# A two-layer cross-attention kernel: a new order inside each beat on all engines, with the transposes of the probabilities ahead of the next scores

## The chip, the cores and the metric

The kernel runs on one core of one Trainium2 chip. The metric is the device time of one execution in microseconds (us).

## The reference

`x` is (64, 128, 160) and `ctx` (64, 77, 256), in fp32. Layer 0 is a transformer block with 20 heads of 64 columns, layer 1 an attention with 20 heads of 8 columns and four image tokens:

```
n = LN1(x);  x = x + attn(n, n)            # a = 0: 128 keys
n = LN2(x);  x = x + attn(n, ctx)          # a = 1: 77 keys
x = (h_a * gelu(h_g)) @ w2 + b2 + x        # h = LN3(x) @ w1 + b1, 640 + 640 columns
# layer 1, context split in 73 text and 4 image tokens:
P = softmax(q k_text / sqrt(8));  text = P v_text
sem = l2norm(P @ text_ctx) . l2norm(image_ctx)
ip = softmax(q k_ip / sqrt(8) + 0.5 sem) * mask @ v_ip
out = (text + ip) @ W_out + b_out + x
```

## The kernel before

The batch is cut into 16 groups (GROUPS) of four batch elements (GB), and each group into two halves (h) of two. In layer 0 a unit n is one pair of heads of one half: n = 0 to 19 are the 128-key attention, 20 to 39 the 77-key one. Two units make a duo d, so a group has 20 duos, and each duo has one **beat**. A beat has three slots t (STEP = 60 slots for a group); every engine runs the same loop `for t in range(FIRST, LAST)` over slots, with `beat, sub = divmod(t, 3)` (`part` on TensorE), and waits only on semaphores. In beat B TensorE transposes the probabilities of duo B (`probs_transposed`), makes the scores of duo B+1 (`scores`), the products with v of duo B-1 (`probs_v`) and the out-projection of duo B-1 (`wo`), and the queries of duo B+2. Layer 1 is cut into 20 units a group too, each of four heads, and one runs in each beat, about one group behind (L1_BEAT): `scores1`, `probs_transposed1`, `probs_v1` on TensorE, `exp1` and `pt1_out` on ScalarE, `softmax1_in` and `unit_out` on VectorE, `norms_of` on GpSimd.

Softmax of a duo: `softmax_in` (VectorE, maximum from PS, L1231), `exp` twice (ScalarE, L977, eight activations in all), `prob_sums` twice (VectorE, L1248 and L1253), `normalise` twice (GpSimd, L1433), transposes (TensorE, L793), `pt_out` (ScalarE, L965). `scores1` writes bank 1 of PT and `probs_transposed1` bank 0, the same two banks that `probs_transposed` fills; so the latter waits for `exp1_done` and `pts1_done`.

Everything else is a **job**: it takes one of the two banks of PG in turn and waits until the job two before it has been read out:

```
if JOB[name] >= len(PG):
    pe.wait_ge(*read_out(JOBS[JOB[name] - len(PG)]))
ps = bank(name)
```

Jobs of every beat are two `qk` (queries, and keys for a = 0; read out by ScalarE, L913) and one `v` (read out by VectorE). Jobs at slots of their own are `xT` (transposes of a norm's output, L659, into nT), `cT` (of the context, L653), `kc` (context keys), `ff` (a feed-forward tile: Gelu on ScalarE, L922, then h on VectorE, L1175), `down`, `q1`, `k1`, `vip`, `ctx1`, and `ipT`, `ip`, `oT1`, `y` at the end of each layer-1 batch element. Their slots stand in tables written by hand at the top (NORM_SLOT for statistics of norm k, half h; FF_SLOT, DOWN_SLOT, Q1_SLOT, PREP_SLOT for the context). Negative slots lie in the group before, those from 60 on in the group behind. SyncE issues all loads in the order of the slots: slices of weights (`load_slice`), stacks, `load_context`, `load_x`.

Of the kernel before, what the change touches and what calls it, by code (L numbers as in the profile page):

```python
# [5 lines left out]
def xattn_program(nc: bass.Bass, D, out: bass.AP):  # L6
    fp32 = mybir.dt.float32
# [55 lines left out]
    FIRST_NORM_SLOT = {(0, 0): -14}  # L63
    VIP_SLOT = 56
    K1_SLOT = (46, 49)
    K1_STACK = 56
    CTX1_SLOT = {0: 59, 1: 74, 2: 89, 3: 104}

    ctx = ExitStack()
    with ctx:  # L70
# [44 lines left out]
        cin, gl = shared[0:TS, :, :], shared[:, :, :]  # L115
# [14 lines left out]
        kx = keys_full[:, :].rearrange("p (a n) -> p a n", a=NP)  # L130
        SE = sb("SE", [128, 4, 512])
# [37 lines left out]
        csq = k1_hi[0:TS, 0, :, :].rearrange("p b t -> p (b t)")[:, 0:E].bitcast(fp32)  # L169
# [184 lines left out]
        def norm_slot(g, k, h):  # L354
            own = FIRST_NORM_SLOT if g == 0 else {}
            return STEP * g + own.get((k, h), NORM_SLOT[(k, h)])

# [5 lines left out]
        tails_at = slots((tail_slot(g, b) + d, (g, b, d)) for g in range(GROUPS) for b in range(GB) for d in range(-1, 9))  # L363

        contexts_at = slots((max(FIRST, STEP * g + (PREP_SLOT[0] + 4 if h else FF_SLOT[-1] + 1 - STEP)), (g, h))
                            for g in range(GROUPS) for h in range(2))
# [14 lines left out]
            + [(tail_slot(g, b) + d, (kind, g, b)) for d, kind in ((5, "ipT"), (6, "ip"), (7, "oT1"), (8, "y"))  # L381
# [86 lines left out]
        with nc.Block() as block:  # L468
# [7 lines left out]
            def _(sp):  # L476
                def load_context(g, h):
                    if h == 0 and g >= 1:
                        sp.wait_ge(S["h_done"], NTH[("ff", g - 1, 2 * F - 1)])
                    elif h == 1:  # L480
                        sp.wait_ge(S["job_full"], JOB[("cT", g, 0)] + 1)
# [57 lines left out]
                for t in range(FIRST, LAST):  # L539
# [40 lines left out]
                    for g, b, d in tails_at(t - 1):  # L580
                        if d == 8:
                            store(g, b)
# [8 lines left out]
            def _(pe):  # L591
# [271 lines left out]
                for t in range(FIRST, LAST):  # L863
                    beat, part = divmod(t, 3)
                    turned, multiplied = min(max(beat + 1, 0), DUOS * GROUPS), min(max(beat, 0), DUOS * GROUPS)
                    if part == 0:
                        if duo_at(beat + 1):
                            scores(*duo_at(beat + 1))
                        if duo_at(beat):
                            probs_transposed(*duo_at(beat))  # L870
                        if duo_at(beat - 1):
                            probs_v(*duo_at(beat - 1))
                    for name in qk_at(t):
                        job(name)
                    for name in late_at(t):
                        if name[0] == "v":
                            job(name)
                    if part == 1 and l1_at(beat - 1):
                        probs_transposed1(*l1_at(beat - 1), turned)
                    if part == 1 and l1_at(beat):  # L880
                        scores1(*l1_at(beat), turned)
                    if part == 2 and duo_at(beat - 1):
                        g, d = duo_at(beat - 1)
                        wo(g, 2 * d)
                        wo(g, 2 * d + 1)
                    if part == 2 and l1_at(beat - 1):
                        probs_v1(*l1_at(beat - 1), multiplied)
                    for name in late_at(t):
                        if name[0] != "v":
                            job(name)  # L890

            @block.scalar
            def _(act):
# [105 lines left out]
                def context_squares(g, h):  # L999

                    act.wait_ge(S["c_in"], 32 * (2 * g + h + 1))
                    if g + h:
                        act.wait_ge(S["c_dve"], HB * (2 * g + h))
                    if g > 0:
                        for w in range(W1):
                            act.wait_ge(S[f"k1_in{w}"], 16 * 3 * g)
# [29 lines left out]
                for t in range(FIRST, LAST):  # L1036
                    beat, sub = divmod(t, 3)
                    if sub == 0 and l1_at(beat - 1):
                        exp1(*l1_at(beat - 1))
                    if sub == 0 and duo_at(beat):  # L1040
                        pt_out(*duo_at(beat))
                    if sub < 2 and duo_at(beat + 1):
                        g, d = duo_at(beat + 1)
                        exp(g, 2 * d + sub)
                    for name in qk_at(t):
                        job(name)
                    if sub == 0 and duo_at(beat - 1):
# [12 lines left out]
                    for kind, i in makes_at(t):  # L1060
                        slice_high(kind, i)
                    for i in splits_at(t):
                        split_high(i)

            @block.vector
            def _(dve):
# [188 lines left out]
                def unit_out(g, n):  # L1255
# [18 lines left out]
                    v.tensor_tensor(gp, o[:, :, D1:D1 + TT], gp, ALU.mult).then_inc(S["on_done"], 1)  # L1274
                    dve.wait_ge(S["on_done"], j)
# [69 lines left out]
                for t in range(FIRST, LAST):  # L1345
# [3 lines left out]
                    if sub == 1 and duo_at(beat + 1):  # L1349
                        g, d = duo_at(beat + 1)  # L1350
                        prob_sums(g, 2 * d)
                    for name in qk_at(t):
                        if name[0] == "kc":
                            job(name)
                    for name in late_at(t):
                        if name[0] == "v":
                            job(name)
                    if sub == 1 and duo_at(beat + 1):
                        g, d = duo_at(beat + 1)
                        prob_sums(g, 2 * d + 1)  # L1360
                    if sub == 2 and l1_at(beat):
                        softmax1_in(*l1_at(beat))
                    if sub == 2 and duo_at(beat - 1):
                        g, d = duo_at(beat - 1)
                        if (2 * d + 1) % NP == NP - 1:
                            block_out(g, 2 * d + 1)
                    if sub == 2 and l1_at(beat - 1):
                        unit_out(*l1_at(beat - 1))
                    for g, h in preps_at(t - 2):
                        context_scale(g, h)  # L1370
                    for name in late_at(t):
                        if name[0] != "v":
                            job(name)
# [3 lines left out]
                    for g, k, h in norms_at(t - 2):  # L1377
                        if k < 3:
                            norm_out(g, k, h)
                    for g, k, h in norms_at(t):  # L1380
                        if k < 3:
                            norm_stats(g, k, h)
                    for g, b, part in tails_at(t):
# [10 lines left out]
            def _(pool):  # L1394
# [52 lines left out]
                for t in range(FIRST, LAST):  # L1447
# [11 lines left out]
                    for g, k, h in norms_at(t - 1):  # L1459
# [10 lines left out]
                    if sub == 2 and l1_at(beat - 1):  # L1470
                        norms_of(*l1_at(beat - 1))
# [28 lines left out]
```

## Time and profile before

| what | value |
|---|---|
| median of 2 runs | 4316.11 us (4306.78 to 4325.45) |
| profiled execution | 4322.96 us |
| its span | 4321.2 us |
| mean granted TensorE clock | 0.935 |
| busy: TensorE, VectorE, ScalarE, GpSimd | 84%, 59%, 56%, 31% |
| chain that ended last: TensorE, VectorE, ScalarE, issue | 56%, 22%, 12%, 10% |
| HBM over the span | 65 GB/s |

Busy shares are means over the span. Weight loads of TensorE (PEld) have rows of their own and overlap its matmuls. "Idle before" is the time that an engine stood still just ahead of a group of instructions, with the engine and the line that released it; "issue" there means that the profile shows no instruction as the releaser.

### The profile page before, as it was taken

Reading aid. Unit: us, or ns where it says so; the run is one execution under the profiler, and the core shown is the slowest. Engines: PE = TensorE matmul, PEld = TensorE weight load, DVE = VectorE, ACT = ScalarE, POOL = GpSimd, SP = SyncE. Lnnn points to the kernel's source line nnn. Section 1 sums busy time; section 2 is a strip of 40 time slices with the busy share of each in tenths; the row PEclk is TensorE's granted clock in tenths of the full one; section 3 lists DMA queues with packets and bytes.
Section 4 is the critical chain, followed back from the end, with each engine's and each line's share of the span. In section 5 each row is a group of like instructions: output and inputs, shape, how many; then the busy total and the mean of one; then the engine's idle time right before and its main releaser. Section 6 shows DMA issues by size and latency. Waiting matters only on the chain.

```text
span 4321.2 us, 96000 instructions
## 1 busy us (share of the span) xinstructions
PE 3645.5 (84%) x34752; PEld 3346.6 (77%) x34752; DVE 2540.2 (59%) x7677; ACT 2432.8 (56%) x6547; POOL 1337.3 (31%) x1657
## 2 busy tenths in 40 slices
PE   6889888888888988889788898888889888897887
PEld 5778778787777878878787787877778787787876
DVE  6546565565656656565565555656566565655654
ACT  4465555555555565565555655555555655655553
POOL 2223332333333323333233323333333233332322
PEclk8999999999999999999999989999999999999985
DMA  5422212222221312213122121322213222131210
GB/s 157 138 60 85 73 50 89 56 86 68 61 88 50 98 57 74 84 46 94 52 88 71 50 89 54 91 66 61 88 49 95 58 73 84 43 98 51 81 41 9
DMA packets 210732, 313.83 MB, mean 73 GB/s; under 512 B 31232, under 2 KB 167520, under 8 KB 210272
## 3 DMA queue, kind: packets, MB, share of 16 engines
q1 hardware_dynamic: 209984, 307.53, 24.3%
q8 instruction: 289, 4.73, 0.5%
q14 instruction: 171, 1.40, 0.1%
q10 hardware_dynamic: 288, 0.16, 0.0%
HBM read 267.97 MB, written 14.42 MB: 65 GB/s over the span
## 4 chain that ended last, share of the span: by engine, by line
PE 56%; DVE 22%; ACT 12%; issue 10%; POOL 0%; DMA 0%; SPq 0%; DVEq 0%; ACTq 0%; POOLq 0%
PE PG L623 7%; PE PW L755 5%; PE PV L809 5%; PE PS L775 5%; PE PG L598 4%; PE PV L858 4%; ACT SE L977 4%; PE PG L615 4%; PE PT L793 4%; DVE mx L1231 3%; PE PG L599 2%; PE PG L601 2%; PE PG L600 2%; PE PT L841 2%; PE PG L699 2%
## 5 line engine op out<-in xcount | busy, mean ns | idle before, releaser
L1433 POOL TENSOR_TENSOR SE<-SE,rs 128x512 f32<-128x512 f32 (+1 forms) x640 | 558.8, 873 | 2016.0 <-DVE rs L1253 2016.0
L977 ACT ACTIVATE SE<-PS,mx 128x77 f32<-128x77 f32 (+1 forms) x2560 | 677.6, 360 | 141.6 <-DVE mx L1231 140.2
L1426 POOL TENSOR_TENSOR n<-qq,p_half 128x4 f32<-128x4 f32 x320 | 323.4, 1010 | 688.8 <-DVE qq L1276 688.8
L965 ACT ACTIVATE PTs<-PT 128x1024 f32<-128x1024 f32 (+1 forms) x320 | 327.0, 1022 | 365.1 <-PE PT L793 365.1
L1169 DVE COPY v_sb<-PG 128x512 f32<-128x512 f32 (+1 forms) x320 | 220.5, 689 | 376.2 <-PE PG L623 219.3
L1248 DVE TENSOR_REDUCE sums<-SE 128x4 f32<-128x512 f32 (+1 forms) x640 | 365.7, 571 | 120.8 <-ACT SE L977 119.3
L995 ACT ACTIVATE SE<-PT,mx 128x73 f32<-128x73 f32 x1280 | 304.5, 325 | 208.8 <-DVE mx L1240 157.8
L755 PE MATMUL PW<-w_o,OTs 128*128 128x160 f32 x2560 | 404.8, 301 | 0.0
L913 ACT ACTIVATE qk<-PG 128x512 f32<-128x512 f32 (+1 forms) x640 | 328.6, 513 | 116.1 <-PE PG L601 109.7
L809 PE MATMUL PV<-PTs,v_sb 128*64 128x128 f32 (+1 forms) x5120 | 392.9, 301 | 0.0
L793 PE MATMUL PT<-ident,SE 64*128 64x64 f32 (+1 forms) x5120 | 255.8, 244 | 160.1 <-issue 155.0
L986 ACT ACTIVATE later<-PT 73x512 f32<-73x512 f32 x320 | 191.6, 599 | 323.0 <-PE PT L841 323.0
L793 PEld LDWEIGHTS PT<-ident,SE 64*128 64x128 f32 (+1 forms) x5120 | 223.4, 155 | 193.1 <-issue 189.0
L755 PEld LDWEIGHTS PW<-w_o,OTs 128*128 128x128 f32 x2560 | 366.9, 191 | 0.0
L858 PE MATMUL PV<-later 73*128 73x86 f32 x2560 | 344.4, 279 | 6.8 <-ACT later L986 6.8
L858 PEld LDWEIGHTS PV<-later 73*128 73x128 f32 x2560 | 333.5, 199 | 12.6 <-ACT later L986 12.6
L623 PE MATMUL PG<-vc_slice,cT 128*77 128x256 f32 x1920 | 277.0, 297 | 72.7 <-DVE later L1175 48.0
L1175 DVE SCALAR_TENSOR_TENSOR later<-PG,b,shared 128x256 f32<-128x256 f32 x160 | 76.4, 482 | 432.9 <-ACT shared L922 425.6
L598 PE MATMUL PG<-nT,q_slice 128*128 128x256 f32 x640 | 242.3, 379 | 102.3 <-DVE nT L1158 45.8
L809 PEld LDWEIGHTS PV<-PTs,v_sb 128*64 128x64 f32 (+1 forms) x5120 | 308.5, 150 | 24.3 <-issue 0.2
L1231 DVE TENSOR_REDUCE mx<-PS 128x8 f32<-128x1024 f32 (+1 forms) x320 | 322.0, 1006 | 8.6 <-PE PS L775 5.5
L623 PEld LDWEIGHTS PG<-vc_slice,cT 128*77 128x77 f32 x1920 | 244.0, 155 | 91.8 <-DVE later L1175 54.7
(207 smaller groups left out, 8800.4 us busy)
## 6 DMA issues: line engine op xcount, KB each, us to landing
q_slice<-q_split SPq DMA_DIRECT2D x630, 192.0 KB, 2.4
vc_slice<-vc_split SPq DMA_DIRECT2D x155, 512.0 KB, 3.7
kc_slice<-kc_split SPq DMA_DIRECT2D x150, 256.0 KB, 2.7
q1st<-q_hi SPq DMA_DIRECT2D x320, 32.0 KB, 1.8
k1st<-k_hi SPq DMA_DIRECT2D x160, 38.5 KB, 2.2
xres<-in_x_dram SPq DMA_DIRECT2D x32, 160.0 KB, 2.4
q1st<-q_lo SPq DMA_DIRECT2D x160, 32.0 KB, 1.9
out_dram<-x SPq DMA_DIRECT2D x64, 80.0 KB, 1.9
```

The lines of the kernel that those rows point to most:

```text
L598: mm(ps, w[0][:, c0:c0 + 128], nT[:, b, 0, :], start=True, stop=False)
L623: last = mm(ps, cT[:, g % 2, c, hc, TS * b:TS * b + rows], w[:, c, hw, c0:c0 + n], start=(c == 0 and i == 0), stop=(c == 1 and i == 2))
L755: last = mm(PW[:, C * b:C * b + C], OTs[:, n % 2, 128 * b:128 * b + 128], w_o[n // U0][:, p, :], start=(p == 0 and b == 0), stop=(p == NP ...
L793: last = tr(PT[0:J, r, at:at + 64], SE[rows, n % 4, J * i:J * i + J], ident[rows, rows])
L809: last = mm(PV[DH * e:DH * e + DH, HT * u + 128 * b:HT * u + 128 * b + 128], v_sb[0:J, d % 2, b, 2 * u + e, :], PTs[0:J, q % 2, u, at:at + ...
L858: last = mm(PV[:, GV * i + off:GV * i + off + GS + D1], PTs1[0:TT, 128 * i:128 * i + 128], gv[:, b % 2, 2 * w + i // 2, off:off + GS + D1] ...
L913: a_(qk[:, i % 2, 0:w, :].rearrange("p a n -> p (a n)"), ps[:, 0:w * HT], ACT.Copy)\
L965: a_(PTs[0:J, q % 2, :, :].rearrange("p u (i r k) -> p r (u i) k", r=2, k=64), PT[0:J, :, :].rearrange("p r (x k) -> p r x k", k=64), ACT. ...
L977: last = a_(SE[:, n % 4, J * i:J * i + J], PS[:, e, J * at:J * at + J], ACT.Exp, bias=mx[:, q % 2, 4 * e + at:4 * e + at + 1])
L1231: v.tensor_reduce(mx[:, q % 2, :].rearrange("p (e x) -> p e x", e=2), PS[:, :, 0:4 * J].rearrange("p e (x j) -> p e x j", j=J), AX, ALU.ma ...
L1248: v.tensor_reduce(sums[:, n % 2, :], SE[:, n % 4, 0:4 * J].rearrange("p (i j) -> p i j", j=J), AX, ALU.add)\
L1433: gp.tensor_tensor(e, e, rs[:, n % 2, :].unsqueeze(2).to_broadcast([128, 4, J]), ALU.mult)\
```

## The change

It leaves every computation as it is and changes its order. (1) TensorE: in slot 0 `probs_transposed(B)` goes ahead of `scores(B+1)`; in slot 1 `probs_transposed1` and `scores1` go ahead of the second `qk` job and of v; in slot 2 `probs_v1` goes ahead of `wo`. (2) ScalarE: `exp1` goes from the head of the next beat to slot 2 of its own; `pt_out` is first in slot 0 and `pt1_out` first in slot 1, ahead of the second `exp`. (3) VectorE: `softmax1_in` goes from slot 2 to slot 1, between the two `prob_sums`; the second `prob_sums` goes ahead of the v copy; the last reduction of `unit_out` becomes `unit_norms`, one beat later; norms and the context's scaling go from the end of a slot to its head. (4) GpSimd: `rstd_of` and `add_bias` are one slot earlier, `norms_of` one beat later. (5) Nearly all slots of the tables move; a norm's output comes three slots behind its statistics, not two, and its transposes five (four for k = 2), not three. (6) L1_BEAT is one beat later. (7) `gl` and `csq` lie in parts of `kx`, so that `cin` is alone in `shared`, and `load_context` waits for the last `cT` job and no longer for the feed-forward.

```diff
-    NORM_SLOT = {(0, 0): -16, (0, 1): -1, (1, 0): 17, (1, 1): 32, (2, 0): 47, (2, 1): 62, (3, 0): 56, (3, 1): 71}
-    FF_SLOT = [51, 52, 53, 53, 54, 66, 67, 68, 68, 69]
-    DOWN_SLOT = [55, 70]
-    Q1_SLOT = [58, 73]
-    PREP_SLOT = [14, 20]
-    X_SLOT = [11, 57]
-    L1_BEAT = BEATS + 1
+    NORM_SLOT = {(0, 0): 42, (0, 1): 3, (1, 0): 18, (1, 1): 33, (2, 0): 48, (2, 1): 69, (3, 0): 60, (3, 1): 84}
+    NEXT_GROUP = {(0, 0)}
+    TURN_AFTER = [5, 5, 4, 1]
+    FF_SLOT = [53, 53, 53, 56, 56, 74, 74, 74, 77, 77]
+    DOWN_SLOT = [59, 80]
+    Q1_SLOT = [62, 86]
+    PREP_SLOT = [-5, 13]
+    CONTEXT_SLOT = [-12, 0]
+    X_SLOT = [24, 60]
+    L1_BEAT = BEATS + 2
...
-    FIRST_NORM_SLOT = {(0, 0): -14}
+    FIRST_NORM_SLOT = {(0, 0): 45}
-    K1_SLOT = (46, 49)
-    K1_STACK = 56
-    CTX1_SLOT = {0: 59, 1: 74, 2: 89, 3: 104}
+    K1_SLOT = (47, 50)
+    K1_STACK = 59
+    CTX1_SLOT = {0: 65, 1: 80, 2: 95, 3: 110}
+    TAIL_JOB = {"ipT": 7, "ip": 9, "oT1": 10, "y": 12}
...
+        gl = kx[:, 0:2, 0:HT]
-        csq = k1_hi[0:TS, 0, :, :].rearrange("p b t -> p (b t)")[:, 0:E].bitcast(fp32)
+        csq = kx[0:TS, NP - 1, 0:E]
...
-            + [(t + (1 if k == 3 else 3), ("xT", g, k, h)) for t, g, k, h in NORMS]
+            + [(t + TURN_AFTER[k], ("xT", g, k, h)) for t, g, k, h in NORMS]
-            + [(STEP * g + PREP_SLOT[h] + 3, ("cT", g, h)) for g in range(GROUPS) for h in range(2)]
+            + [(STEP * g + PREP_SLOT[h] + 4, ("cT", g, h)) for g in range(GROUPS) for h in range(2)]
...
                     if part == 0:
+                        if duo_at(beat):
+                            probs_transposed(*duo_at(beat))
                         if duo_at(beat + 1):
                             scores(*duo_at(beat + 1))
-                        if duo_at(beat):
-                            probs_transposed(*duo_at(beat))
                         if duo_at(beat - 1):
                             probs_v(*duo_at(beat - 1))
+                    if part == 1 and l1_at(beat - 1):
+                        probs_transposed1(*l1_at(beat - 1), turned)
+                    if part == 1 and l1_at(beat):
+                        scores1(*l1_at(beat), turned)
                     for name in qk_at(t):
                         job(name)
                     for name in late_at(t):
                         if name[0] == "v":
                             job(name)
-                    if part == 1 and l1_at(beat - 1):
-                        probs_transposed1(*l1_at(beat - 1), turned)
-                    if part == 1 and l1_at(beat):
-                        scores1(*l1_at(beat), turned)
+                    if part == 2 and l1_at(beat - 1):
+                        probs_v1(*l1_at(beat - 1), multiplied)
...
-                    if part == 2 and l1_at(beat - 1):
-                        probs_v1(*l1_at(beat - 1), multiplied)
...
-                    if sub == 0 and l1_at(beat - 1):
-                        exp1(*l1_at(beat - 1))
                     if sub == 0 and duo_at(beat):
                         pt_out(*duo_at(beat))
+                    if sub == 1 and l1_at(beat - 1):
+                        pt1_out(*l1_at(beat - 1))
                     if sub < 2 and duo_at(beat + 1):
                         g, d = duo_at(beat + 1)
                         exp(g, 2 * d + sub)
...
-                    if sub == 1 and l1_at(beat - 1):
-                        pt1_out(*l1_at(beat - 1))
+                    if sub == 2 and l1_at(beat):
+                        exp1(*l1_at(beat))
```

## Rows read from the trace of the kernel before

**Rows 1.** The page's first part: busy time, share of the span, instructions, by engine.
```profile
PE 3645.5 (84%) x34752; PEld 3346.6 (77%) x34752; DVE 2540.2 (59%) x7677; ACT 2432.8 (56%) x6547; POOL 1337.3 (31%) x1657
```

**Rows 2.** The view of the cores: span and mean granted clock.
```profile
core 0: 4321.2 us, clock 0.935
```

**Rows 3.** The list of waits, TensorE's: total us, times, longest.
```profile
PE PT L793 <- issue: 155.0, 208, 1.8
...
PE PG L659 <- DVE nx L1115: 116.5, 96, 13.6
...
PE PG L623 <- DVE later L1175: 48.0, 31, 2.0
PE PG L598 <- DVE nT L1158: 47.8, 30, 1.7
...
PE PG L598 <- ACT qk L913: 45.3, 82, 0.8
PE PG L653 <- DVE shared L1137: 44.9, 32, 2.4
PE PG L606 <- DVE later L1175: 43.9, 30, 1.6
PE PG L728 <- ACT qk L913: 38.8, 28, 1.6
...
PE PG L606 <- ACT qk L913: 28.5, 26, 1.6
...
PE PG L623 <- ACT qk L913: 18.0, 12, 2.6
```

**Rows 4.** Timeline, head of a 77-column beat: start, duration, engine, line, what.
```profile
2000.99 0.96 ACT L995 ACTIVATE SE<-PT,mx 128x73 f32<-128x73 f32 x4 [1.06 <-DVE mx L1240]
2001.16 0.97 PEld L775 LDWEIGHTS PS<-kx,qk 64*128 64x128 f32 x16
...
2002.05 0.64 PEld L793 LDWEIGHTS PT<-ident,SE 64*77 64x77 f32 x16
```

**Rows 5.** Windows: stretch, length, busy time by engine, granted clock, DMA, GB/s.
```profile
2245.30:2256.10 10.80, 10.30 (x115) 9.65 (x114) 6.63 (x22) 5.29 (x17) 2.62 (x5) 1.00 0.40 135
2507.60:2521.00 13.40, 13.00 (x114) 12.16 (x115) 6.62 (x22) 5.53 (x17) 2.60 (x5) 0.78 0.34 109
...
2504.00:2508.00 4.00, 2.63 (x34) 2.18 (x33) 3.89 (x14) 1.45 (x5) 1.67 (x2) 0.84 0.21 87
...
4151.00:4321.00 170.00, 126.50 (x669) 110.29 (x669) 79.69 (x316) 63.89 (x177) 43.71 (x53) 0.61 0.04 11
```

**Rows 6.** Timeline of a 128-column beat.
```profile
2177.93 1.22 DVE L1231 TENSOR_REDUCE mx<-PS 128x8 f32<-128x1024 f32 x1
...
2179.18 1.14 ACT L977 ACTIVATE SE<-PS,mx 128x128 f32<-128x128 f32 x4 [1.12 <-DVE mx L1231]
...
2179.86 0.19 PEld L598 LDWEIGHTS PG<-nT,q_slice 128*128 128x128 f32 x1
...
2181.15 1.17 ACT L977 ACTIVATE SE<-PS,mx 128x128 f32<-128x128 f32 x4
...
2181.79 0.48 PEld L841 LDWEIGHTS PT<-ident,SE 128*73 128x73 f32 x4
...
2182.35 1.15 PEld L755 LDWEIGHTS PW<-w_o,OTs 128*128 128x128 f32 x8
...
2182.72 0.68 DVE L1248 TENSOR_REDUCE sums<-SE 128x4 f32<-128x512 f32 x1
...
2183.69 1.07 POOL L1433 TENSOR_TENSOR SE<-SE,rs 128x512 f32<-128x512 f32 x1 [1.32 <-DVE rs L1253]
```

**Rows 7.** Groups by line: the table loads of the Gelu line.
```profile
L922 ACT ACT_TABLE_LOAD x95 | 121.9, 1283 | 1.7
```

**Rows 8.** Timeline, a Gelu and the load ahead of it.
```profile
2320.71 1.28 ACT L922 ACT_TABLE_LOAD   x1
...
2322.01 0.47 ACT L922 ACTIVATE shared<-PG,b 128x256 f32<-128x256 f32 x1
```

More of the change, by code:

```diff
@@ L355, in norm_slot @@
             own = FIRST_NORM_SLOT if g == 0 else {}
-            return STEP * g + own.get((k, h), NORM_SLOT[(k, h)])
+            return STEP * (g - ((k, h) in NEXT_GROUP)) + own.get((k, h), NORM_SLOT[(k, h)])
         NORMS = sorted((norm_slot(g, k, h), g, k, h) for g in range(GROUPS) for k, h in NORM_SLOT)
@@ L362, in xattn_program @@
         preps_at = slots((STEP * g + PREP_SLOT[h], (g, h)) for g in range(GROUPS) for h in range(2))
-        tails_at = slots((tail_slot(g, b) + d, (g, b, d)) for g in range(GROUPS) for b in range(GB) for d in range(-1, 9))
-        contexts_at = slots((max(FIRST, STEP * g + (PREP_SLOT[0] + 4 if h else FF_SLOT[-1] + 1 - STEP)), (g, h))
-                            for g in range(GROUPS) for h in range(2))
+        tails_at = slots((tail_slot(g, b) + d, (g, b, d)) for g in range(GROUPS) for b in range(GB) for d in range(-1, 13))
+        contexts_at = slots((max(FIRST, STEP * g + CONTEXT_SLOT[h]), (g, h)) for g in range(GROUPS) for h in range(2))
         splits_at = slots((s, i) for i, s in enumerate(SPLIT_SLOT))
@@ L377, in xattn_program @@
             [(STEP * g + 3 * d + 1, ("v", g, d)) for g in range(GROUPS) for d in range(DUOS)]
[L378 removed]
+            + [(t + TURN_AFTER[k], ("xT", g, k, h)) for t, g, k, h in NORMS]
             + [(STEP * g + Q1_SLOT[h], ("q1", g, h)) for g in range(GROUPS) for h in range(2)]
[L380 to L381 removed]
+            + [(STEP * g + PREP_SLOT[h] + 4, ("cT", g, h)) for g in range(GROUPS) for h in range(2)]
+            + [(tail_slot(g, b) + d, (kind, g, b)) for kind, d in TAIL_JOB.items()
                for g in range(GROUPS) for b in range(GB)]
@@ L477, in load_context @@
                 def load_context(g, h):
[L478 to L481, printed above, removed]
+                    if g + h:
+                        sp.wait_ge(S["job_full"], JOB[("cT", g if h else g - 1, 1 - h)] + 1)
                     for rows, t0, t1 in ((slice(0, T), 0, T), (slice(T, T + NIP), TT, T)):
@@ L1348, in _ @@
                         softmax_in(*duo_at(beat + 1))
[L1349 to L1368, printed above, removed]
+                    if sub == 0 and l1_at(beat - 2):
+                        unit_norms(*l1_at(beat - 2))
                     for g, h in preps_at(t - 2):
                         context_scale(g, h)
-                    for name in late_at(t):
-                        if name[0] != "v":
-                            job(name)
                     for g, k, h in norms_at(t):
@@ L1376, in _ @@
                             l1_input(g, h)
-                    for g, k, h in norms_at(t - 2):
+                    for g, k, h in norms_at(t - 3):
                         if k < 3:
@@ L1382, in _ @@
                             norm_stats(g, k, h)
+                    if sub == 1 and duo_at(beat + 1):
+                        g, d = duo_at(beat + 1)
+                        prob_sums(g, 2 * d)
+                    if sub == 1 and l1_at(beat):
+                        softmax1_in(*l1_at(beat))
+                    for name in qk_at(t):
+                        if name[0] == "kc":
+                            job(name)
+                    if sub == 1 and duo_at(beat + 1):
+                        g, d = duo_at(beat + 1)
+                        prob_sums(g, 2 * d + 1)
+                    for name in late_at(t):
+                        if name[0] == "v":
+                            job(name)
+                    if sub == 2 and l1_at(beat - 1):
+                        unit_out(*l1_at(beat - 1))
+                    if sub == 2 and duo_at(beat - 1):
+                        g, d = duo_at(beat - 1)
+                        if (2 * d + 1) % NP == NP - 1:
+                            block_out(g, 2 * d + 1)
+                    for name in late_at(t):
+                        if name[0] != "v":
+                            job(name)
                     for g, b, part in tails_at(t):
@@ L1458, in _ @@
                         normalise(g, 2 * d + 1)
-                    for g, k, h in norms_at(t - 1):
+                    for g, k, h in norms_at(t):
                         if k < 3:
@@ L1469, in _ @@
                         gp.tensor_tensor(cst[:, 1, :], cst[:, 0, :], p_half[0:TS, 0:HB], ALU.pow).then_inc(S["c_pow"], 1)
-                    if sub == 2 and l1_at(beat - 1):
-                        norms_of(*l1_at(beat - 1))
+                    if sub == 0 and l1_at(beat - 2):
+                        norms_of(*l1_at(beat - 2))
 _INS = ['x', 'ctx_2048', 'fside_S_0',
```

11 lines of the change are left out of this document (6 added, 5 removed).

## The prediction

> **What bounds the kernel now.** I read the page's first part, then the mean clock, the list of waits, and last the timeline of single beats. TensorE is busy 84% of the span and no other engine passes 59%, so the time is TensorE's work plus its gaps [rows 1]. Its granted clock averages 0.935 [rows 2]; as there are two levels, 1.2 and 2.4 GHz, that is (1 - 0.935) x 2 x 4321 = 562 us at the lower one. The list of waits shows who ends TensorE's gaps [rows 3]; the ten rows add up to 587 us, in four kinds:
> - A, 155.0 us: the transposes of the probabilities (L793). The timeline shows why [rows 4]. The scores of the next duo go ahead of them; then they stop until ScalarE's second-layer exponentials (L995) end at 2000.99 + 0.96 = 2001.95, and start at 2002.05. They do not read these results: the second layer's scores lie in a bank of PT that the transposes overwrite.
> - B, 116.5 + 44.9 = 161.4 us: transposes of normalised rows (L659) and of the context (L653), which wait for VectorE.
> - C, 48.0 + 43.9 + 47.8 = 139.7 us: jobs behind the feed-forward (L623 and L606 wait for a PG bank until VectorE has made h) and behind the low part of nT (L598).
> - D, 45.3 + 38.8 + 28.5 + 18.0 = 130.6 us: a job that waits for its PG bank until ScalarE has copied the queries out (L913). There are two banks, so a job needs the read-out of the job two before it.
>
> A gap is paid a second time. In 2504 to 2508 us TensorE worked 2.63 of 4.00 us, and the beat around and behind it ran at a mean clock of 0.78 and took 13.4 us; the same beat of the group before, at 1.00, took 10.8 [rows 5]. The lower level lasted (1 - 0.78) x 2 x 13.4 = 5.9 us there, so one us of it cost 2.6 / 5.9 = 0.44 us. I take 0.4. The last 170 us ran at 0.61, which is 133 us at the lower level; this stretch holds almost only second-layer units, and I leave it. 429 us lie in the groups.
>
> **The change part by part.** There are 16 groups. The sum starts from the profiled execution, 4323 us, which lies 0.2% over the median of 4316; I do not correct for that.
>
> 1. TensorE runs the transposes before the next scores, and the second-layer scores, maximum and exponentials come one or two thirds of a beat earlier on TensorE, VectorE and ScalarE. Then exp1 has ended before the head of the next beat, and A goes. What is late next is the softmax itself, worked out for a 128-column beat from its own timeline [rows 6]. Count from the start of the transposes. The scores start at 0.65 and load for 0.97 [rows 4]; I add 0.25 for the last result and the hand-over, so the maximum starts at 1.9. The first exponentials follow 1.25 later (2177.93 to 2179.18), at 3.2. The second set starts 1.97 later today (2179.18 to 2181.15: four exponentials, the query copy, the OTs copy). The change puts the copy of PTs1 ahead of it, about 0.5 as the OTs copy; so it starts at 5.6 and, with its 1.17, ends at 6.8. The sums start at once, and sums, reciprocal and GpSimd's product take (2183.69 + 1.07) - 2182.72 = 2.04. The next transposes can start at 8.9 to 9.0. TensorE's own work in such a beat is 6.0 up to the end of v (part 4) and some 2.1 for the two products behind it (the eight WO matmuls ran from 2182.35, 1.1, and PV1's eight are taken as long): 8.1. So only beats with hardly any extra work wait, at some 0.9 us. I keep 25 us of A; bounds are 0 and 155. Term: -130.
>
> 2. Norms are taken out three slots behind the statistics and turned five behind (four for k = 2), not two and three; the context gets one slot more, and both stand at the head of VectorE's slot. A slot is a third of a beat, 3.6 us of one of 10.8 [rows 5]; two more are some 7 us. The wait of today is 116.5 us over 96 normalisations [rows 3], or 1.2 us each. These instructions (bn_stats, nx) are queued behind the maximum and ahead of prob_sums, which has to wait for exponentials anyway; today they stand at the slot's end and push the next maximum. I keep 7 us of B: -154. If something else is late the bound is 0. The wait for x_done in norm_stats is at the head of VectorE's queue with prob_sums behind it, but block_out stands one slot earlier there.
>
> 3. The feed-forward is now done in runs of 3 and 2 at the end of two beats. The three of a run need two banks, so the third waits for VectorE's h. ScalarE's exp1 is ahead of the Gelus, so I put 0.75 us on each of two such waits, and on the jobs behind the pairs as much: 50 us of C stay, -90; bounds 0 and -140. Loads of activation tables drop as well: the 95 loads for Gelu [rows 7] are 3 per half group and become 2, with as many for the way back: 4 per group at 1.283 us, 82 us of ScalarE in all. It hides behind the wait for h and the softmax, so it is already in C; I add 0 and keep 82 for the low end. In the timeline the load starts at 2320.71 and the Gelu at 2322.01 [rows 8], 1.30 later. The Trainium skill (ScalarE: Activation LUTs, What ACT_TABLE_LOAD costs) adds a drain of about 1.38 us and so 2.66 us for each switch, which would make 170 us of the 82; this trace shows no such drain behind the load.
>
> 4. The jobs of slot 1. In new order T1, S1, second queries, v, extra jobs; the products PV1 and WO come behind. An extra job needs the bank of the second queries, whose copy stands behind the second exponentials. ScalarE: these start at 5.6, and four of them and the copy end at 7.3. TensorE: 0.64 for the transposes and 0.97 for the scores [rows 4], no more than 0.9 for the PV products, 2181.79 - 2179.86 = 1.93 for the second queries and v, half of that for the first queries, and 2182.35 - 2181.79 = 0.56 for T1 and S1 [rows 6]: 6.0. So it waits 1.3 us. By the slots, seven 128-column beats of a group have such a job (xT, ip or y), two 77-column ones at 0.6, and four beats with kc jobs wait 0.2: 7 x 1.3 + 1.2 + 0.8 = 11.1 us, 178 in all against 130.6: +47. Bounds: 0 wait (-130), and the whole of ScalarE's row below.
>
> 5. The lower clock. 25 + 7 + 50 + 178 = 260 us of 587 stay. In proportion 239 of the 429 us would go, worth 96; but waits of about 1 us stay in most 128-column beats, so I take 60. Bounds 0 and -170.
>
> 6. L1_BEAT is one later: one more second-layer unit at the end. The tail row shows 170 us for some 21 beats, with their jobs [rows 5]; a bare one is shorter: +5. Bounds 0 and +8. The k = 3 norms and q1 move to slots 84 and 86, well ahead of their first unit.
>
> 7. The rest I cost at nothing. Moving gl and csq into kx drops ScalarE's wait for the k1 stacks. SyncE's context loads move to slots -12 and 0; they wait on a context transpose that stands one beat or more earlier, and the q, kc and vc slices and stores queued behind them have two to three slots. If that cover failed, I would put a slot, a third of the 10.8 us beat [rows 5], on each group: 58 us.
>
> Sum: 4323 - 130 - 154 - 90 + 47 - 60 + 5 = 3941, said as 3940.
>
> **The rivals.**
> - R1, the softmax takes A's place. The longer way through scores, maximum, exponentials, PTs1 copy, sums and product binds in most 128-column beats, because late copies of the beat before push it. For it: the way is 9.0 against 8.1 us. Against: most such beats carry one to four us of extra jobs. A gives back 100 of its 130 and the clock its 60: 3940 + 160 = 4100.
> - R2, the gaps go and the clock follows. The table loads were on the path (-82), the clock gives its 96 (-36), the bank waits are half (-89): about 3735.
> - R3, slower: the bank wait of part 4. If TensorE comes to the extra job when ScalarE has only begun the first exponentials, it waits from 3.2 to 7.3, 4.1 us, in 11 beats of each group: 722 instead of 178 us, and 4485 us. It eats the whole gain from 3.2 us a beat, and is slower by 2% from 3.6. For it: the PV1 and WO products stand behind this job now and no longer cover it. Against: v itself cannot start before the first query copy, so TensorE cannot be that early. The Trainium skill speaks for R3: in Perfetto Trace Analysis, Matmuls, independent groups are to rotate through PSUM banks so that the read-out of one lies under the next group, and the same page calls repeated gaps a sign of too few buffers; the change adds no bank.
> - R4, the change does not do what it says: A becomes a wait for GpSimd at the same place and B and C only move: 4315, within 2%.
>
> **How the numbers follow.** Forecast 0.55, R1 0.22, R2 0.10, R3 0.06, R4 0.07. 2% is about what a measurement of this kernel can tell from no change: faster means under 4230, slower over 4402. Forecast, R2 and most of R1 (0.20 of 0.22) are faster: 0.85; R4 and the rest of R1 the same: 0.09; R3 slower: 0.06. The forecast's own bounds are 3800 (C all gone, bank waits half) and 4060 (bank waits double). The range must take in R2's upper half and R1: 3770 to 4180.
>
> **What would show it.** Right: L793 waits under 40 us in all; L659 and L653 under 20 together; table loads about 130, not 191; a mean clock of 0.945 to 0.96; waits for L913 as the largest kind, in front of L659, L731 and L740 in the middle of a beat; a group of 234 to 238 us in place of some 4151 / 16 = 259. Wrong: L793 behind L1433 by more than 100 us (R1); waits for L913 of over 500 us (R3); the clock above 0.97 with waits under 150 us (R2); waits of L598 or L623 for slices from DMA, which now have next to none.

## The result, and the profile after

The changed kernel takes 3642.85 us (median of two runs, 3630.58 to 3655.11): 0.844 of the time before, with a 95% interval of 0.8295 to 0.8585. The forecast was 3940 us, with 3770 as its lower end. Faster was right; the size was not.

First the page's first part of the changed kernel, against [rows 1]:

```profile
PE 3388.8 (93%) x34752; PEld 3148.5 (87%) x34752; DVE 2443.0 (67%) x7677; ACT 2301.6 (63%) x6485; POOL 1328.8 (37%) x1657
```

and the view of its cores, against [rows 2]:

```profile
core 0: 3628.8 us, clock 0.981
```

The same 34752 matmuls are busy 257 us less, and the span has 3628.8 - 3388.8 = 240 us without one, where it had 4321.2 - 3645.5 = 676. So the 692 us came in two parts: 436 us of gaps and 257 us of busy time. Most of the second part has a cause in the other row: (1 - 0.981) x 2 x 3628.8 = 138 us at the lower clock level, and 562 before.

The list of waits, TensorE's own, against [rows 3] (line numbers are two higher: L661 is the transposing of norms, L795 that of probabilities, L617 the first keys of layer 1 (k1), L733 is ip, L742 y, L915 the query copy):

```profile
PE PG L661 <- ACT qk L915: 23.9, 30, 0.8
PE PG L733 <- ACT qk L915: 23.8, 28, 0.9
PE PG L742 <- ACT qk L915: 22.2, 28, 0.8
...
PE PG L617 <- DVE nT L1157: 21.7, 14, 1.6
PE PT L795 <- POOL SE L1440: 20.0, 40, 3.7
PE PG L600 <- DVE cipT L1150: 19.2, 15, 1.4
...
PE PG L661 <- DVE nx L1114: 15.8, 2, 13.2
PE PG L625 <- ACT qk L915: 12.9, 46, 0.4
...
PE PG L608 <- ACT qk L915: 12.3, 32, 0.9
```

Kind A went from 155.0 to 20.0 us, and what releases the transposes is now the softmax itself (GpSimd's product). B is 15.8, of which one wait at the start is 13.2. The five rows of the query copy (kind D) add up to 95 us, and no wait in them is longer than 0.9.

A 128-column beat in the timeline (start, duration, engine, line, what), against [rows 6]:

```profile
1754.86 0.57 PEld L795 LDWEIGHTS PT<-ident,SE 64*128 64x128 f32 x16 [0.17 <-issue]
...
1756.57 1.22 DVE L1230 TENSOR_REDUCE mx<-PS 128x8 f32<-128x1024 f32 x1 [0.69 <-PE PS L777]
...
1757.83 1.14 ACT L979 ACTIVATE SE<-PS,mx 128x128 f32<-128x128 f32 x4 [1.19 <-DVE mx L1230]
...
1759.79 0.61 ACT L988 ACTIVATE later<-PT 73x512 f32<-73x512 f32 x1
...
1760.27 1.15 ACT L979 ACTIVATE SE<-PS,mx 128x128 f32<-128x128 f32 x4
...
1761.27 0.64 ACT L915 ACTIVATE qk<-PG 128x512 f32<-128x512 f32 x1
...
1761.96 0.66 PE L661 MATMUL PG<-ident,nx 128*128 128x128 f32 x4 [0.80 <-ACT qk L915]
...
1763.15 0.95 ACT L997 ACTIVATE SE<-PT,mx 128x73 f32<-128x73 f32 x4
...
1765.59 0.57 PEld L795 LDWEIGHTS PT<-ident,SE 64*128 64x128 f32 x16 [0.19 <-issue]
```

The maximum starts 1.71 us behind the transposes, the exponentials 2.97 and 5.41, and the bank is free at 7.05 (1761.27 + 0.64); the prediction had 1.9, 3.2, 5.6 and 7.3. The second layer's exponentials (L997) end at 1764.10, 1.5 us ahead of the next transposes, and no longer hold them.

Windows of the changed kernel (stretch, length, busy time by engine, granted clock), three beats on end of one group, a whole group, with that beat near its end, two stretches at the same place of two groups, and the last 170 us, against [rows 5]:

```profile
1439.80:1451.70 11.90, 11.62 (x121) 10.80 (x123) 7.48 (x27) 6.45 (x21) 4.96 (x7) 1.00 0.42 125
1451.70:1462.70 11.00, 10.71 (x111) 10.02 (x111) 7.36 (x23) 5.92 (x19) 3.10 (x4) 1.00 0.49 141
1462.70:1470.40 7.70, 7.70 (x91) 7.28 (x93) 5.83 (x19) 5.12 (x18) 3.06 (x4) 1.00 0.39 120
1554.62:1773.93 219.31, 207.74 (x2175) 193.59 (x2174) 149.96 (x475) 141.99 (x402) 82.51 (x103) 1.00 0.29 86
1041.00:1053.00 12.00, 10.45 (x86) 9.69 (x85) 5.97 (x19) 6.17 (x20) 3.60 (x5) 0.72 0.18 64
1484.50:1496.50 12.00, 10.36 (x108) 9.58 (x107) 7.68 (x26) 6.41 (x21) 4.78 (x7) 1.00 0.36 114
3459.00:3629.00 170.00, 143.39 (x973) 128.21 (x971) 98.47 (x392) 83.02 (x231) 55.95 (x69) 0.75 0.09 25
```

Gaps of 0.3 us are left in the first two, and the clock stays at 1.00. It does so in the whole group from 1554.62, the beat with the wait of 0.80 included. The last 170 us hold (1 - 0.75) x 2 x 170 = 85 of the 138 us at the lower level, so 53 are left in front of them, where the kernel before had 429. Between 200 and 3459 us the clock falls only four times, each time behind the wait of the k1 job (L617, 14 times 1.55 us); behind the other ten of these equal waits it stays up. The stretches from 1041.00 and from 1484.50 show one of each.

The groups by line show the table loads, against [rows 7]:

```profile
L924 ACT ACT_TABLE_LOAD x64 | 82.1, 1283 | 1.1
L979 ACT ACT_TABLE_LOAD x61 | 78.3, 1283 | 1.1
L997 ACT ACT_TABLE_LOAD x2 | 2.6, 1283 | 2.4 <-DVE sip L1242 2.4
```

### The profile page after: what moved, and what is told of

It reads as the page before. It is cut to its first block and busy times, and to the rows that moved or that the text cites. A ratio compares the mean times of both kernels' runs of the same rounds, so it can differ in the third digit from the quotient of the medians.

```text
span 3628.8 us, 95846 instructions
## 1 busy us (share of the span) xinstructions
PE 3388.8 (93%) x34752; PEld 3148.5 (87%) x34752; DVE 2443.0 (67%) x7677; ACT 2301.6 (63%) x6485; POOL 1328.8 (37%) x1657
## 3 DMA queue, kind: packets, MB, share of 16 engines
q1 hardware_dynamic: 209984, 307.53, 28.9%
## 5 line engine op out<-in xcount | busy, mean ns | idle before, releaser
L757 PEld LDWEIGHTS PW<-w_o,OTs 128*128 128x128 f32 x2560 | 358.9, 191 | 0.0
L811 PE MATMUL PV<-PTs,v_sb 128*64 128x128 f32 (+1 forms) x5120 | 354.6, 281 | 0.0
L915 ACT ACTIVATE qk<-PG 128x512 f32<-128x512 f32 (+1 forms) x640 | 328.0, 513 | 12.2 <-PE PG L603 12.2
L997 ACT ACTIVATE SE<-PT,mx 128x73 f32<-128x73 f32 x1280 | 310.2, 350 | 9.6 <-DVE sip L1242 9.6
L811 PEld LDWEIGHTS PV<-PTs,v_sb 128*64 128x64 f32 (+1 forms) x5120 | 276.5, 138 | 32.3 <-issue 0.4
L625 PE MATMUL PG<-vc_slice,cT 128*77 128x256 f32 x1920 | 255.8, 282 | 17.2 <-ACT qk L915 12.9
L795 PEld LDWEIGHTS PT<-ident,SE 64*128 64x128 f32 (+1 forms) x5120 | 197.0, 142 | 80.3 <-issue 54.1
L795 PE MATMUL PT<-ident,SE 64*128 64x64 f32 (+1 forms) x5120 | 244.7, 233 | 20.5 <-POOL SE L1440 20.0
L625 PEld LDWEIGHTS PG<-vc_slice,cT 128*77 128x77 f32 x1920 | 228.5, 146 | 30.9 <-ACT qk L915 26.2
L1412 POOL TENSOR_SCALAR vp<-mv 128x2 f32<-128x2 f32 x96 | 39.2, 409 | 524.9 <-DVE mv L1097 524.9
L600 PE MATMUL PG<-nT,q_slice 128*128 128x256 f32 x640 | 216.3, 338 | 11.6 <-DVE w_k_rem L1314 7.7
L1450 POOL TENSOR_TENSOR kbd<-k1st,head_of_row 96x308 fp32r<-96x308 f32 x320 | 223.4, 698 | 0.0
```

Source lines behind the costliest of these rows:

```text
L625: last = mm(ps, cT[:, g % 2, c, hc, TS * b:TS * b + rows], w[:, c, hw, c0:c0 + n], start=(c == 0 and i == 0), stop=(c == 1 and i == 2))
L757: last = mm(PW[:, C * b:C * b + C], OTs[:, n % 2, 128 * b:128 * b + 128], w_o[n // U0][:, p, :], start=(p == 0 and b == 0), stop=(p == NP ...
L795: last = tr(PT[0:J, r, at:at + 64], SE[rows, n % 4, J * i:J * i + J], ident[rows, rows])
L811: last = mm(PV[DH * e:DH * e + DH, HT * u + 128 * b:HT * u + 128 * b + 128], v_sb[0:J, d % 2, b, 2 * u + e, :], PTs[0:J, q % 2, u, at:at + ...
L915: a_(qk[:, i % 2, 0:w, :].rearrange("p a n -> p (a n)"), ps[:, 0:w * HT], ACT.Copy)\
```

## The experiments

All were timed beside the kernel before. A ratio is given with its 95% interval. "Not busy" is the span less TensorE's busy time of the page's first part, "lower" is (1 - clock) x 2 x span. These two, the busy time and the clock belong to the profiled execution, not to the median; for e3 it was the slowest one (3685 us), and the clock of its three others was 0.984 or 0.985.

| kernel | median us | ratio, interval | not busy | PE busy | clock | lower |
|---|---|---|---|---|---|---|
| before | 4316 | 1 | 676 | 3645.5 | 0.935 | 562 |
| changed | 3643 | 0.844 (0.8295 to 0.8585) | 240 | 3388.8 | 0.981 | 138 |
| e1 tables | 4017 | 0.930 (0.925 to 0.935) | 447 | 3550.7 | 0.952 | 384 |
| e2 order | 4035 | 0.934 (0.930 to 0.937) | 527 | 3504.1 | 0.962 | 306 |
| e3 scores first | 3663 | 0.849 (0.845 to 0.853) | 267 | 3416.1 | 0.976 | 177 |
| e4 fill xT | 4286 | 0.993 (0.990 to 0.996) | 620 | 3681.4 | 0.947 | 456 |
| e5 turn 3 | 3659 | 0.849 (0.848 to 0.851) | 269 | 3388.4 | 0.984 | 117 |
| e6 copy first | 3572 | 0.829 (0.828 to 0.830) | 210 | 3359.9 | 0.981 | 136 |
| e7 ff spread | 3754 | 0.871 (0.870 to 0.873) | 311 | 3442.9 | 0.967 | 248 |
| e8 delay | 4011 | 0.931 (0.928 to 0.933) | 458 | 3559.1 | 0.947 | 426 |
| e9 norms end | 3650 | 0.844 (0.842 to 0.846) | 246 | 3409.9 | 0.974 | 190 |
| e10 exp1 late | 4346 | 1.005 (1.003 to 1.007) | 674 | 3648.9 | 0.915 | 735 |
| e11 swap only | 4852 | 1.122 (1.120 to 1.124) | 899 | 3954.1 | 0.858 | 1378 |
| e12 copy first, k1 | 3544 | 0.820 (0.818 to 0.821) | 190 | 3351.8 | 0.982 | 128 |

**e1, the tables alone; e2, the order alone.** e1 is the changed kernel with the four slot loops of the kernel before; e2 the kernel before with the four new loops:

```diff
# e2, in the new loops, as the old slots need it:
+    for g, k, h in norms_at(t - 2):   # norm_out, at the end of VectorE's slot
-    for g, k, h in norms_at(t):
+    for g, k, h in norms_at(t - 1):   # rstd_of, add_bias on GpSimd
```

> The changed kernel with the four old orders inside a beat (TensorE, ScalarE, VectorE, GpSimd), and the new slots of all jobs. If the parts are worth what the prediction gives them: kinds B and C of the waits go and A stays, 4323 - 154 - 90 = 4080 us for the gaps alone. If the clock follows the gaps far better than the prediction took (theory K): some 250 us less of the lower level, another 120 to 150 us, so 3930 to 3960. Rival W, that tables help only together with the new order: over 4200.

> The kernel before with the new order inside a beat on all engines, but the old slots; norms and the context's scaling stay at the end of VectorE's slot as they were. Kind A goes, the bank waits grow: 4323 - 130 + 47 = 4240 us for the gaps; under K the clock adds only some 30 us, as B and C still bring it down: 4200. Rival W: over 4250 as well, and the two halves together then add up to far less than the 680 us of the whole.

Each half is worth about 0.07: 299 us and 281 us. Together they would be 580, and the change gives 673, so some 93 us belong to neither alone (the interval of the changed kernel alone is 63 us to either side). The waits of e1:

```profile
PE PT L795 <- issue: 202.5, 250, 2.0
```

and of e2:

```profile
PE PG L659 <- DVE nx L1115: 123.6, 81, 14.5
...
PE PG L653 <- DVE shared L1137: 50.6, 32, 2.5
```

The kinds split: the tables end B and leave A (even more of it), the order ends A and leaves B. Theory K was too hopeful for e1 by 60 us and not hopeful enough for e2 by 165; as to W, neither half is near to nothing alone. One thing the totals hide: e1 took away more idle time than e2 (447 us are left in e1, 527 in e2), yet e2 spends less time at the lower level (306 us, and e1 384). So the clock did not follow the sum of the gaps.

**e3, scores ahead of the transposes again in the changed kernel.**

```diff
-    probs_transposed(*duo_at(beat))
     scores(*duo_at(beat + 1))
+    probs_transposed(*duo_at(beat))
```

> The changed kernel with only the scores put back ahead of the transposes in slot 0. By the working of part 1 the maximum starts 0.65 us earlier, while the transposes have nothing left to wait for; the first exponentials come at 2.7, not 3.2, and the bank waits of the 128-column beats shrink by up to 0.5 us in seven beats a group: 3590 to 3640 us. Rival: the transposes at the head are what carries the change, and without them the time is over 3750 us, as PTs come one microsecond later.

Both theories missed. It is not faster, and it does not cost 100 us; against the changed kernel the intervals overlap. So the swap of transposes and scores is by itself worth nothing that these runs can tell. Its bank waits are 121 us for 95 in the five rows (L733 28.9 for 23.8, L608 25.8 for 12.3). One of its 128-column beats shows why the exponentials come no earlier:

```profile
302.59 0.97 PEld L777 LDWEIGHTS PS<-qk 64*128 64x128 f32 x16 [0.17 <-issue]
...
303.84 0.43 DVE L1157 TENSOR_TENSOR nT<-PG,nT 64x256 fp32r<-64x256 f32 x1
...
304.30 1.22 DVE L1230 TENSOR_REDUCE mx<-PS 128x8 f32<-128x1024 f32 x1
...
305.55 1.14 ACT L979 ACTIVATE SE<-PS,mx 128x128 f32<-128x128 f32 x4 [0.24 <-DVE mx L1230]
```

The scores stand at the head, but the maximum now finds VectorE busy with a read-out of the beat before (L1157) and starts 1.71 behind the head, the exponentials 2.96, as in the changed kernel (1.71 and 2.97). Over its 115 beats of this kind without a table load the medians are 1.61 and 2.86, a gain of 0.1 in place of 0.5.

**e11, the same swap alone in the kernel before.**

> The kernel before with the transposes put ahead of the scores and nothing else. The exponentials of the second layer still stand at ScalarE's head, so the transposes wait for them in place of standing behind 1 us of scores: the gap grows by up to 1 us in the 208 beats that have it and appears in others: 100 to 250 us more, 4400 to 4550 us. Rival: the earlier transposes shorten the softmax path, and the time falls below 4250 us.

12% slower, more than expected. The head of one beat in its timeline (a Gelu's table load stands ahead in this one):

```profile
2308.93 0.96 ACT L995 ACTIVATE SE<-PT,mx 128x73 f32<-128x73 f32 x4
2309.95 0.66 PEld L793 LDWEIGHTS PT<-ident,SE 64*77 64x77 f32 x16 [3.06 <-issue]
...
2310.50 1.00 PEld L775 LDWEIGHTS PS<-kx,qk 64*128 64x128 f32 x16
```

With exp1 at the beat's head the scores were the cover for this wait: L793's wait goes from 155.0 to 437.0 us in the list, and the lower clock from 562 to 1378 us.

**e10, only the second layer's exponentials late again.**

```diff
+    if sub == 0 and l1_at(beat - 1):
+        exp1(*l1_at(beat - 1))
     if sub == 0 and duo_at(beat):
         pt_out(*duo_at(beat))
-    if sub == 2 and l1_at(beat):
-        exp1(*l1_at(beat))
```

> The changed kernel with the second layer's exponentials alone put back to the head of the next beat on ScalarE, ahead of pt_out; maximum and scores stay early. Kind A comes back, and now the scores do not stand ahead of the transposes to cover part of it: 0.5 to 1 us in most of 320 beats, 160 to 300 us, and the clock with it, 60 to 150 us: 3850 to 4050 us. Rival: ScalarE is idle between the beats and runs them ahead of time, so the wait does not return: under 3720 us.

This one call takes back the whole gain, with all the new slots and the rest of the order in place: 4346 us, clock 0.915, some 300 us more than the top of what was expected. Two beats of its timeline:

```profile
2098.84 0.96 ACT L997 ACTIVATE SE<-PT,mx 128x73 f32<-128x73 f32 x4
...
2099.87 0.60 PEld L795 LDWEIGHTS PT<-ident,SE 64*128 64x128 f32 x16 [1.79 <-issue]
...
2106.78 1.00 ACT L997 ACTIVATE SE<-PT,mx 128x73 f32<-128x73 f32 x4
...
2108.31 0.35 PEld L795 LDWEIGHTS PT<-ident,SE 64*128 64x128 f32 x8 [0.36 <-issue]
```

In the first the exponentials end at 2099.80 and the transposes start at 2099.87. Its waits, against 20.0 us in the changed kernel:

```profile
PE PT L795 <- issue: 426.5, 223, 2.9
```

So e10 and e11 together show what the swap needs: transposes may stand first only where exp1 has already left their bank.

**e4, idle transposes in the gap of kind B, kernel before.**

```diff
 elif kind == "xT":
+    if name[2] < 3 and g > 0:
+        for _ in range(9):
+            tr(ps[:, 0:128], ident[:, :], ident[:, :])
     pe.wait_ge(S["nx_done"], NORM[name[1:]] + 1)
```

> The kernel before with nine idle transposes of the identity (some 1.05 us) put ahead of each transposing of a norm's output, in the bank that this job has already got, in groups 1 to 15. They lie in the gap of kind B (about 1.2 us, 90 times), which stays as long as it was; only its idle part is filled. Theory K (gaps cost mostly through the clock that falls behind them): the mean clock rises from 0.935 to 0.945 or more, and the time falls by 30 to 80 us. Rival P (TensorE's busy time shrank for another reason, such as a better packing of matmuls in the new order): clock and time as before, 4310 to 4330 us, or 20 us more.

810 matmuls of useless work make the kernel 0.7% faster (30 us). The clock rises from 0.935 to 0.947, and the lower level lasts 106 us less. No other work was moved; the gap is only filled. So the clock follows a filled gap, and P, as it was put for this run, does not hold. For the change itself P is not refuted: part of the fall in busy time is not the clock's (see below, step 5).

**e8, one more microsecond on ScalarE in each beat.**

```diff
 def ot_out(g, d):
+    for _ in range(4):          # each waits for the one before
+        a_(spare[:, :], ident[:, 0:64], ACT.Copy)
```

> The changed kernel with four small chained copies (some 1 us in all) on ScalarE ahead of its OTs copy in every beat. They lengthen the way to the second exponentials and to the bank's release by the same time. Theory K, with a clock that falls only behind longer gaps: the gaps of 0.3 to 0.8 us become 1.3 to 1.8 us, idle time grows by 150 to 300 us, and on top the time at the lower level grows from 137 to 350 us or more, so 3850 to 4050 us in all. Rival: the clock does not mind such gaps spread one to a beat, stays at 0.975 or more, and the time grows by the idle time alone.

From its timeline, the added copies and the job behind the query copy:

```profile
2000.76 1.15 ACT L961 ACTIVATE spare<-ident 128x64 f32<-128x64 f32 x4
2001.82 0.58 ACT L966 ACTIVATE OTs<-PV 128x512 f32<-128x512 f32 x1
2003.78 0.61 ACT L916 ACTIVATE qk<-PG 128x512 f32<-128x512 f32 x1
2004.44 0.66 PE L662 MATMUL PG<-ident,nx 128*128 128x128 f32 x4 [1.89 <-ACT qk L916]
```

The gap of 0.80 has become 1.89. Not busy grows by 218 us, and the lower level from 138 to 426; K was right, in size too. The span grew by 388 us: 218 of gaps and 170 of busy time for the same 34752 matmuls.

**e5, e9: what ended kind B.** e5 has `TURN_AFTER = [3, 3, 3, 1]`; e9 moves VectorE's norm and context calls behind its late jobs.

> The changed kernel with the transposes of a norm's output only three slots behind its statistics, as before, not five or four; the output itself stays three slots behind. If kind B was as big as the prediction put it, and the clock comes with the gaps (theory K): 90 waits of 1 to 2 us, 110 to 170 us, and 60 to 100 us through the clock, so 3790 to 3900 us. Rival: the wait for VectorE lies under the bank wait of the same slot and costs little: under 3690 us.

> The changed kernel with VectorE's norm and context work (norm statistics and output, l1 input, context scaling) put back at the end of its slot, at the same slots as in the change. e5 showed that the two slots more for the transposes are worth only some 16 us, so something else ended kind B. If it is this place at the head of the slot, behind the maximum, the maximum of a duo now waits for norm work again: 3720 to 3800 us. Rival: it is the free slack of the new order and the place is worth nothing: 3630 to 3670 us.

The rival holds both times. In e5 the wait is back (L661 behind nx 72.1 us, 80 times), but the one for the bank shrinks from 23.9 to 12.1, and the time is 3659 for 3643. Without the one at the start that is 57 us, where the kernel before had 103: the two slots do end more than half of kind B, and it is worth 16 us at most. These waits are 0.7 us each, and from 200 to 3480 us the clock does not leave 1.00. e9 is the changed kernel within the interval, so VectorE's place alone is worth nothing that can be told.

**e7, the feed-forward spread as before.**

```diff
-    FF_SLOT = [53, 53, 53, 56, 56, 74, 74, 74, 77, 77]
+    FF_SLOT = [53, 54, 55, 55, 56, 74, 75, 76, 76, 77]
```

> The changed kernel with the feed-forward jobs spread over four slots in turn (53, 54, 55, 55, 56 and 74, 75, 76, 76, 77), as before, in place of runs of 3 and 2. Table loads go back from about 8 to 12 a group, 64 more at 1.283 us, 82 us of ScalarE. The prediction cost them at nothing beside the waits for h; if that holds, 3640 to 3690 us. Rival: they stand in the softmax path and count in full, with the clock behind them: 3720 to 3800 us.

In each half three of the five feed-forward jobs move by one or two slots, so that only two of them share a slot. The rival holds: 111 us more. Table loads of its groups by line, 249 against 127 in the three rows shown above:

```profile
L924 ACT ACT_TABLE_LOAD x125 | 160.4, 1283 | 2.2
L979 ACT ACT_TABLE_LOAD x92 | 118.0, 1283 | 1.6
L997 ACT ACT_TABLE_LOAD x32 | 41.1, 1283 | 1.5 <-DVE sip L1242 1.0
```

That is 122 loads more, not the 64 that I had counted, and 157 us of ScalarE for 111 us of time. A beat shows them on the path:

```profile
503.69 1.28 ACT L924 ACT_TABLE_LOAD   x1
...
508.93 0.58 PE L600 MATMUL PG<-nT,w_hi 128*128 128x256 f32 x1 [1.63 <-ACT qk L915]
```

Between the two ScalarE runs the Gelu (504.98), a second load at 505.96, the exponentials (507.25) and the query copy (508.27), for which TensorE waits. This edit also moves the jobs among the banks, so the 111 us are not the loads' alone.

**e6 and e12: the query copy ahead of the second exponentials.**

```diff
+    if sub == 1:
+        for name in qk_at(t):
+            job(name)
     if sub < 2 and duo_at(beat + 1):
         g, d = duo_at(beat + 1)
         exp(g, 2 * d + sub)
-    for name in qk_at(t):
-        job(name)
+    if sub != 1:
+        for name in qk_at(t):
+            job(name)
# e12 also:
-    K1_SLOT = (47, 50)
+    K1_SLOT = (46, 50)
```

> The changed kernel with ScalarE's copy of the second queries ahead of the second exponentials, not behind them. Theory of part 4 of the prediction: the bank waits of the slot-1 jobs (L661, L733, L742 behind L915, some 70 us) end, the exponentials come 0.5 us later, which only the light beats feel (16 to 48 us): 3590 to 3640 us. Rival: the softmax path is the real limit of the 128-column beats, and half a microsecond in each of 320 beats adds 100 us or more: over 3740 us.

> e6 with the first k1 job one slot earlier (46, not 47), so that it no longer takes the bank of the norm's transposes in the same slot. In the trace of e6 that job is the largest single gap of a group, 1.55 us, 14 times, 21.7 us; it goes and little else moves: 3545 to 3560 us. Rival: the gap moves to the next job, 3565 to 3580 us.

In e6's timeline the copy runs at 1737.60 and xT starts with no wait, while the exponentials start 0.48 later:

```profile
1737.60 0.62 ACT L915 ACTIVATE qk<-PG 128x512 f32<-128x512 f32 x1
1737.85 1.04 POOL L1444 TENSOR_TENSOR SE<-SE,rs 128x512 f32<-128x512 f32 x1
1738.08 1.16 ACT L979 ACTIVATE SE<-PS,mx 128x128 f32<-128x128 f32 x4
1738.27 0.42 PEld L661 LDWEIGHTS PG<-ident,nx 128*128 128x128 f32 x4
```

e6 beat its expectation, 71 us under the changed kernel (the two intervals just touch), and the waits for GpSimd grew only from 20.0 to 24.9. e12 takes the k1 gap too, as expected, and is the fastest kernel of this study: 3544 us, 0.820 of the time before and clear of the changed kernel's interval.

## Why the prediction was wrong, by its own steps

- **Step 5, the lower clock, failed, in its amount.** It said that 60 us come back, 150 us of the lower level at 0.4, because waits of about 1 us stay in most 128-column beats and would bring the clock down as before. Waits of 0.8 us and less did stay, in five or six beats of a group, and the groups run at 1.00 around them. Of the 429 us in the groups 53 are left, where the prediction kept 279; with the last 170 us the lower level lost 424 us. e8 shows where the assumption would have held: with gaps of up to 2.1 us in the same beats the level is back at 426.

  The price of 0.4 was right. Two whole groups of the kernel before, with the same matmuls:

```profile
1062.83:1322.24 259.41, 219.12 (x2175) 201.26 (x2173) 156.18 (x476) 150.41 (x407) 82.99 (x102) 0.97 0.25 72
...
2368.64:2636.40 267.76, 231.88 (x2175) 213.71 (x2174) 156.08 (x476) 151.34 (x407) 83.01 (x102) 0.92 0.24 70
```

  Unrounded, they hold 13.7 and 44.4 us at the lower level, so one us of it costs 12.76 / 30.7 = 0.42; a line through twelve groups gives 0.41. A line through 13 kernels (all but e4) gives more, 3332 + 0.467 x lower, with no kernel off by more than 51 us; but the busy time at 1.00 differs between kernels, and such a line mixes that in.

  That difference is a term that the prediction does not have. At 1.00 a group of the kernel before would be busy for 219.12 - 0.41 x 13.7 = 213.5 us, and one of the changed kernel is for 207.7: 5.8 us, or 92 us in 16 groups. In the stretches at 1.00 about 3.0 us of it lie in the scores and 2.5 in the products with the query slices; the other lines nearly cancel. Why is open: better overlap in the new order would look so, and so would a part of a wait that hides under the modelled end of a matmul.
- **Step 4, the bank waits, right in mechanism and twice too large.** 95 us in the five rows for 178 predicted; the wait is 0.8 for 1.3 us. In the beat shown ScalarE freed the bank 0.25 us sooner (7.05 for 7.3), mostly because the scores stand 0.49 behind the transposes and not 0.65, and TensorE came to the job 0.3 later (at 6.3, not 6.0); the PV products, taken at 0.9 or less with no row, took 1.0. Term: some -35 in place of +47. e6 shows the cause directly.
- **Step 1 held**: 20.0 us of A for 25, released by GpSimd's product as said. What it missed is how much hangs on exp1: e10 takes all 700 us back, through waits of 427 us in all and the clock at 0.915. (In its working 6.8 + 2.04 is 8.8, not 8.9 to 9.0; nothing else hangs on it.)
- **Step 2 held in size** (15.8 for 7, of which 13.2 is the kernel's start, and before as well). Of its reasons the two slots show in the waits (57 us come back in e5) but hardly in the time, and VectorE's place in neither (e9).
- **Step 3**: the waits of kind C are now behind nT and cipT (21.7 and 19.2), 41 for 50. The table loads, costed at nothing, are on the path: e7 pays 111 us with 122 loads more. My count of the loads after the change, about 130, was right (129 for 191); what these 62 are worth in the change itself was not measured. The drain of 1.38 us behind each load, which the Trainium skill adds (ScalarE: Activation LUTs, What ACT_TABLE_LOAD costs), found no support here: in e7's beat above the Gelu starts 1.29 us behind the start of its load (503.69 to 504.98), in the changed kernel ScalarE stood idle for 1.1 us in all ahead of the 64 loads of L924, and the 122 loads of e7 cost at most 0.9 us each, less than their own 1.283.
- **Step 6** had the wrong sign: behind the last maximum of layer 0 the changed kernel needs 3628.8 - 3488.3 = 140 us, the one before 4321.2 - 4150.8 = 170. Its last 170 us ran at 0.75, not at 0.61. I had left those 133 us alone as not to be had.
- The ten rows of waits left out 676 - 587 = 89 us of gaps in smaller rows; the sum treated them as fixed, and they are 240 - 172 = 68 now (20.0 of A, 15.8 of B, 41 of C and 95 of D are the 172).
- R1 and R3 did not come. R2 named what did come, gaps that go and a clock that follows, and its sign was nearly there, a clock above 0.97 with waits of 172 us for its 150; but at 3735 us it did not go far enough either.

The sum with the measured sizes: 4321 less 436 of gaps, less 0.41 x 424 = 174 for the clock, less 92 of busy time at 1.00 is 3619, against 3629 measured. The forecast had 327, 60 and nothing for these three, so its miss of some 310 us comes in three parts of like size: 109, 114 and 92. Open stay the cause of the 92 us, what the 62 loads fewer are worth, and what ends the rest of B.

## What to carry to other kernels

Count a gap of the bounding engine twice: its length, and the lower clock behind it, here 0.41 us for each us at that level. Do not scale the second part with the sum of the gaps: some 80 waits of 0.7 us left the clock up from 200 to 3480 us (e5), 14 waits of 1.55 us brought it down four times (changed kernel), and it can go to nearly nothing while gaps stay. Measure the price inside one kernel, on groups that do the same work. Before moving an instruction to the head of a stage, list what every resource it touches still waits for: the swap that is harmless in the changed kernel, and worth nothing that e3 can tell, costs 12% without the earlier exponentials. Where two banks rotate, look at what the read-out is queued behind; one copy moved ahead of four exponentials gave 2%.

## What I had not expected of the hardware

- 810 useless matmuls in a gap made the kernel 30 us faster; the mean clock rose from 0.935 to 0.947 (e4).
- Gaps of 0.8 us in five or six beats of a group leave the granted clock at 1.00 for whole groups; gaps of up to 2.1 us at the same places bring the mean to 0.947 (e8). The same gap of 1.55 us brought it down in four groups and not in ten.
- Moving three of the five feed-forward jobs of each half by one or two slots doubled the activation table loads, 127 to 249 in the rows shown (e7).
